# Merged per-tile orders, gates out of PSUM, fewer gathers and products of zeros in a 16-tile transformer kernel

## The reference

```python
h = ln(word[x] + pos[itok] + type[mask]) * gamma + beta            # E
h = h + relu((linear_attention(ln(h)) @ Wo.T + bo) @ Wfc.T + bfc)  # P: 16 heads, 44 random features each
h = h + experts(ln(h))                     # F: the two nearest of 32 prototypes, products of rank 16
h = h + rotary_attention(ln(h)) @ Wo                               # R: 16 heads, causal softmax
h = h + relu(ln(h) @ q(W1).T + b1) @ q(W2).T + b2                  # M: ternary weights, 256 to 1024 to 256
```

## Time and profile before

| | us |
|---|---|
| runs | 519.41, 523.40, 524.96 (median 523.4) |
| profiled execution | 519.33, with a span of 517.6 |
| TensorE busy | 394.7 (76%) |
| VectorE busy | 377.2 (73%) |
| GpSimd busy | 283.1 (55%) |
| ScalarE busy | 265.2 (51%) |
| mean granted TensorE clock | 0.91 |

### The profile page before, as it was taken

One profiled execution on the slowest core, in us unless ns is written; L12 is line 12 of the kernel. 1 busy time (PEld: TensorE's weight loads), 2 busy tenths in 40 slices (PEclk: granted clock), 3 DMA queues, 4 the chain that ended last, 5 costly groups with the idle time before them and its releaser, 6 DMA issues.

```text
span 517.6 us, 11583 instructions
## 1 busy us (share of the span) xinstructions
PE 394.7 (76%) x3722; PEld 261.4 (51%) x3754; DVE 377.2 (73%) x1026; ACT 265.2 (51%) x547; POOL 283.1 (55%) x380
## 2 busy tenths in 40 slices
PE   4164727587879888888988889889898988866764
PEld 1043414354546555655655557656565666443533
DVE  5254797889596979796969696979797977663231
ACT  2146532537383847474747474747565654624320
POOL 7516364658485758484848484848585534422110
PEclk9775567889897999999999999999999999988896
DMA  5587233464646696969596968886776858462472
GB/s 160 146 221 187 42 61 75 82 115 92 117 93 125 93 166 101 158 107 162 108 162 98 172 105 140 127 166 112 158 123 147 119 120 147 84 133 62 82 119 74
DMA packets 198650, 62.94 MB, mean 122 GB/s; under 512 B 190240, under 2 KB 195648, under 8 KB 198592
## 3 DMA queue, kind: packets, MB, share of 16 engines
q1 hardware_dynamic: 196288, 55.91, 59.1%
q0 software_dynamic: 2304, 6.29, 5.0%
HBM read 13.42 MB, written 2.10 MB: 30 GB/s over the span
## 4 chain that ended last, share of the span: by engine, by line
DVE 20%; POOL 17%; DMA 17%; PE 17%; issue 14%; SPq 12%; ACT 3%; POOLq 0%; DVEq 0%; ACTq 0%
DMA hgT<-hgs 7%; SPq L408 5%; PE PS L1241 5%; POOL stage_f L500 3%; PE PS L1341 3%; PE PS L1399 3%; SPq L418 2%; DMA xTr<-xsr 2%; POOL qe L528 2%; POOL split L508 2%; DMA rT<-split 2%; DMA mT<-stage_r 2%; POOL hres L504 2%; POOL rstdE L489 1%; POOL dist L522 1%
## 5 line engine op out<-in xcount | busy, mean ns | idle before, releaser
L1341 PE MATMUL PS<-w2q,mT 128*128 128x256 f16 x256 | 37.0, 308 | 5.7 <-DMA mT<-stage_r 5.7
L465 POOL TENSOR_TENSOR rstdR<-rstdR,consts 128x1 f32<-128x1 f32 x16 | 8.9, 559 | 55.8 <-DVE rstdR L926 55.8
L880 DVE TENSOR_REDUCE split<-PS 128x16 f16<-128x2048 f32 x16 | 36.5, 2284 | 3.7 <-PE PS L1327 3.7
L1241 PE MATMUL PS<-wqkT_hi,xTP 128*128 128x512 f16 x64 | 26.3, 456 | 14.3 <-DMA xTP<-xsP 14.3
L1318 PE MATMUL PS<-va,kp 128*88 128x34 f32 x256 | 25.6, 260 | 13.4 <-ACT kp L1192 13.4
L1592 PE MATMUL PS<-w1q,xTM 128*128 128x512 f16 x128 | 32.8, 379 | 2.3 <-DMA xTM<-xsM 1.5
L1399 PE MATMUL PS<-faT_hi,hgT 128*128 128x256 f16 x128 | 24.7, 281 | 12.8 <-DMA hgT<-hgs 12.2
L1318 PEld LDWEIGHTS PS<-va,kp 128*88 128x88 f32 x256 | 25.4, 178 | 17.4 <-ACT kp L1192 15.5
L1341 PEld LDWEIGHTS PS<-w2q,mT 128*128 128x128 f16 x256 | 26.9, 110 | 14.0 <-DMA mT<-stage_r 6.8
L1012 ACT ACTIVATE xnR<-hres,nmeanR,rstdR 128x256 f32<-128x256 f32 x16 | 9.6, 601 | 47.3 <-DVE nmeanR L938 47.3
L909 DVE SCALAR_TENSOR_TENSOR qs<-PS,qs 128x512 f16<-128x512 f32 x16 | 11.1, 691 | 28.2 <-ACT qs L1069 28.2
(11 more groups left out here) (282 smaller groups left out, 1428.5 us busy)
## 6 DMA issues: line engine op xcount, KB each, us to landing
out<-outb SPq DMA_DIRECT2D x16, 128.0 KB
w<-in_w1T SPq DMA_DIRECT2D x1, 1024.0 KB, 5.1
w<-in_w2T SPq DMA_DIRECT2D x1, 1024.0 KB, 8.0
stage_p<-in_wqkT SPq DMA_DIRECT2D x1, 512.0 KB, 3.7
stage_f<-in_fbT SPq DMA_DIRECT2D x1, 512.0 KB, 4.3
stage_f<-in_faT SPq DMA_DIRECT2D x1, 512.0 KB, 4.8
stage_r<-in_rwqk SPq DMA_DIRECT2D x1, 512.0 KB, 5.1
rT<-split SPq DMA_TRANSPOSE x32, 3.3
```

What stands on the lines that cost most here:

```text
L880: v.tensor_reduce(slots(48)[:, 0:H, 0].rearrange("p (c j) -> p j c", j=4), PS[:, BANK["mk1"]:BANK["mk1"] + 4, :].rearrange("p j (c k) -> p ...
L1241: last = pe.matmul(dst, xT[x][:, xp, :], wp[:, c, :], start=(n == 0), stop=(n == 3 * KC - 1 and bias is None))
L1341: pe.matmul(PS[:, BANK["m2"], 0:D], mT[:, j, :], w2q[:, j % FC, :], start=(j == 0), stop=False)
```

## The change

The step loop goes. Each engine's list is now all its ops for all 16 tiles, sorted by a place, `START[t] + STRETCH[t] * PLACE[op]`, and run from the first to the last. A place is a number for sorting; nothing waits for it. The semaphore waits are as before, except that TensorE's waits for a bank's earlier readers are written with counters (`issued`, `free`), the statistics use one semaphore less, and the banks are dealt anew. Laid out, the lists overlap more tiles: the gather runs five tiles ahead of fQ where it ran two ahead, and m2 seven behind.

Apart from that:

- Embedding: VectorE adds the two type rows to the 128 position rows once, SyncE writes the 256 x 256 sum to memory, and from tile 1 on each tile gathers from two tables instead of three; e1 is left out (tile 0 keeps three gathers and two adds, its first sum in `escaled`). The first gather of tile 1 waits for the table (`pt_out`).
- Gates: the row 0, 1, ..., 31 is written by a TensorE product into PSUM beside the distances of each tile, and the two comparisons read it there. The copy of the gates' high half goes to ScalarE (gsh, one instruction for both places), the low half to GpSimd (gsl). The sum of the weights and its reciprocal are an op of their own (ws). near moves from GpSimd to VectorE.
- Context: masked in place in PSUM; cth and ctl read it there.
- `keep_warm` issues products of zeros, 128x512 each, ahead of the wait of some products of tiles 0 to 4, into the bank that the product writes next. The entries for s1 in `WARM` are not used; the others are 48 products.

```diff
-LAG = {
-    "g": 0, "e1": 0, "e2": 0, "Est": 0, "Eag": 0, "Ers": 0, "Enm": 0, "Exn": 0,
-    "esc": 0, "eh": 0, "Pst": 0, "Pag": 0, "Prs": 0, "Pnm": 0, "Pxn": 0, "Phi": 0,
...
+FIRST, LAST = 3, 13
+START = (-2.56349, -1.38567, -0.20596, 0.99134, 2.22478, 3.48108, 4.78958, 6.10492, 7.46585, 8.85026, 10.27633, 11.72602, 13.22702, 14.73596, 16.29312, 17.86576)
+STRETCH = (0.87678, 0.89108, 0.90959, 0.9307, 0.95508, 0.97952, 0.99847, 1.02279, 1.04753, 1.07265, 1.09779, 1.12259, 1.14249, 1.16846, 1.20385, 1.2177)
+PLACE = {
+    "g": (-4.57909, -4.57909, -4.57909), "e2": (-3.97764, -3.97764, -3.97764), "Est": (-3.6722, -3.6722, -3.6722), "Eag": (-3.6282, -3.6282, -3.6282),
...
+    "PT": (-2.59489, -2.59489, -2.59489), "qk": (-0.58726, -0.58726, -0.58726), "v": (-0.25364, -0.25364, -0.25364), "qhi": (-0.31092, -0.31092, -0.31092),
...
+ENGINE = {
+    "SP": "PT qT qp onT hgT rT1 rT2 rT3 roT MT mT st".split(),
+    "POOL": "g e2 Ers esc eh Prs Plo qel onl Frs dist gsl hgl Rrs rot rl rol Mrs Mlo".split(),
+    "DVE": "Est Eag Enm Pst Pag Pnm qlo diag kmx kmr kb kd ctxt qmx qb qd ctl od on hP Fst Fag Fnm FT nd2 top near tix gap gt ws hg hF Rst Rag Rnm RT rc rs1 rs2 ngm rd ro hR Mst Mag Mnm ml1 ml2 ob".split(),
+    "ACT": "Exn Pxn Phi qhi sq ke kp va qe1 qe2 cth onh Fxn Fhi xsq tpf sec gsh hgh Rxn Rhi rh1 rh2 rh3 vr ex1 ex2 oh roh Mxn Mhi mh1 mh2".split(),
+    "PE": "qk v fK kmxT kbc ctx fQ o of Ftr prt fh y Rtr rqk rv mk1 s1 mk2 s2 pvx pvT wo m1 m2".split(),
+}
 BANK = {
-    "qk": 0, "kmxT": 2, "kbc": 6, "fK": 4, "v": 2, "ctx": 7, "fQ": 0, "o": 1,
-    "of": 1, "Ftr": 3, "prt": 3, "fh": 2, "y": 7, "Rtr": 7, "rqk": 7, "rv": 7,
-    "mk1": 3, "pvx": 6, "pvT": 7, "wo": 1, "m1": 0, "m2": 2,
+    "qk": 5, "kmxT": 7, "kbc": 6, "fK": 0, "v": 3, "ctx": 6, "fQ": 2, "o": 0,
+    "of": 3, "Ftr": 1, "prt": 7, "fh": 1, "y": 1, "Rtr": 3, "rqk": 3, "rv": 1,
+    "mk1": 4, "pvx": 4, "pvT": 0, "wo": 2, "m1": 2, "m2": 0,
 }
-TERN_BANK = 3
+
+
+WARM = {
+    "fQ": {0: 7, 1: 2},
+    "kmxT": {0: 5},
+    "ctx": {0: 2},
+    "o": {0: 3, 4: 1},
+    "of": {0: 10},
+    "kbc": {1: 1},
+    "Ftr": {0: 2},
+    "y": {0: 4, 2: 2, 3: 2},
+    "fK": {2: 4},
+    "s1": {0: 2, 1: 2},
+    "prt": {2: 1, 3: 2},
+}
+
+TERN_BANK = 4
...
+def due(engine):
+
+    def place(op, t):
+        return START[t] + STRETCH[t] * PLACE[op][0 if t < FIRST else 2 if t >= LAST else 1]
+
+    return sorted(((op, t) for op in ENGINE[engine] for t in range(TILES)), key=lambda x: (place(*x), x[1]))
 
...
-        emb = sb("emb", [P, 3, D])
-        esum1 = sb("esum1", [P, D])
+        emb = sb("emb", [P, 2, D])
+        emb_type = sb("emb_type", [P, D])
...
-        ctxt = sb("ctxt", [MP, HP, 2 * VA])
...
+            get("T", pos_rows, A["pos"])
+            get("T", pt_rows.rearrange("p r n -> p (r n)"), A["type"].partition_broadcast(P))
...
+            sp.wait_ge(pt_ok, 1)
+            sp.dma_start(A["pt"].rearrange("(r p) n -> p r n", p=P), pt_rows).then_inc(pt_out, 16)
...
-            for i in range(LAST_STEP + 1):
-                step(Step(i))
+            for op, t in due("SP"):
+                step(op, t)
...
+                if t == 1:
+                    g.wait_ge(ids_ok, 4)
+                    g.wait_ge(pt_out, 16)
+                tables = ((emb[:, 0, :], A["word"], ids[:, 0, t:t + 1]), (emb[:, 1, :], A["pos"], ids[:, 1, t:t + 1]),
+                          (emb_type[:, :], A["type"].rearrange("(r n) -> r n", n=D), ids[:, 2, t:t + 1]))
+                if t > 0:
+                    tables = (tables[0], (emb[:, 1, :], A["pt"], ids_pt[:, t:t + 1]))
+                for dst, table, rows_ in tables:
+                    g.indirect_dma_start(dst, None, table, bass.IndirectOffsetOnAxis(rows_, 0)).then_inc(g_ok, 16)
...
+                elif op == "gsl":
+                    wait(g, gsh_ok, t + 1)
+                    o = 2 * R2
+                    g.tensor_tensor(hgs[:, o + PROTO:o + 2 * PROTO], gates[:, :], hgs[:, o:o + PROTO], ALU.subtract).then_inc(gsl_ok, 1)
...
-                t = s.tile("gsp")
-                if t is not None:
-                    o = 2 * R2
-                    wait(v, gt_ok, 4 * t + 4)
-                    wait(v, hgT_ok, 16 * t)
-                    v.tensor_copy(hgs[:, o:o + PROTO], gates[:, :]).then_inc(gsp_ok, 1)
-                    v.tensor_copy(hgs[:, o + 2 * PROTO:o + 3 * PROTO], gates[:, :]).then_inc(gsp_ok, 1)
-                    wait(v, gsp_ok, 3 * t + 2)
-                    v.tensor_tensor(hgs[:, o + PROTO:o + 2 * PROTO], gates[:, :], hgs[:, o:o + PROTO], ALU.subtract).then_inc(gsp_ok, 1)
...
+                elif op == "near":
+                    wait(v, top_ok, t + 1)
+                    wait(v, dist_ok, t)
+                    v.tensor_scalar(near[:, :], top[:, 0:2], -1.0, None, ALU.mult).then_inc(near_ok, 1)
...
+                elif op == "ctxt":
+                    wait(v, ctx_ok, t + 1)
+                    ctxt = PS[0:MP, BANK["ctx"], 0:H * VA].rearrange("p (a b) -> p a b", a=HP)
+                    v.tensor_tensor(ctxt, ctxt, pair_mask[:, :, :], ALU.mult).then_inc(ctxt_ok, 1)
+                elif op == "ctl":
+                    wait(v, cth_ok, t + 1)
+                    v.tensor_tensor(ctl[:, :, :], PS[0:MP, BANK["ctx"], 0:H * VA].rearrange("p (a b) -> p a b", a=HP), cth[:, :, :],
+                                    ALU.subtract).then_inc(ctl_ok, 1)
...
+                elif op == "gt":
                     wait(v, sec_ok, t + 1)
                     wait(v, tpf_ok, t + 1)
-                    v.tensor_scalar(wsum[:, 0:1], second[:, :], 1.0, None, ALU.add).then_inc(gt_ok, 1)
-                    v.tensor_scalar(gate1[:, :], iota[:, :], topf[:, 1:2], second[:, 0:1], ALU.is_equal, ALU.mult).then_inc(gt_ok, 1)
-                    wait(v, gt_ok, 4 * t + 2)
-                    v.reciprocal(wsum[:, 1:2], wsum[:, 0:1]).then_inc(gt_ok, 1)
-                    v.scalar_tensor_tensor(out=gates[:, :], in0=iota[:, :], scalar=topf[:, 0:1], in1=gate1[:, :],
+                    wait(v, gsh_ok, t)
+                    wait(v, gsl_ok, t)
+                    order = PS[:, BANK["prt"], PROTO:2 * PROTO]
+                    v.tensor_scalar(gate1[:, :], order, topf[:, 1:2], second[:, 0:1], ALU.is_equal, ALU.mult).then_inc(gt_ok, 1)
+                    wait(v, gt_ok, 2 * t + 1)
+                    v.scalar_tensor_tensor(out=gates[:, :], in0=order, scalar=topf[:, 0:1], in1=gate1[:, :],
                                            op0=ALU.is_equal, op1=ALU.add).then_inc(gt_ok, 1)
...
+                elif op == "ws":
+                    wait(v, sec_ok, t + 1)
+                    v.tensor_scalar(wsum[:, 0:1], second[:, :], 1.0, None, ALU.add).then_inc(ws_ok, 1)
+                    wait(v, ws_ok, 2 * t + 1)
+                    v.reciprocal(wsum[:, 1:2], wsum[:, 0:1]).then_inc(ws_ok, 1)
...
+                elif op == "gsh":
+                    wait(a, gt_ok, 2 * t + 2)
+                    wait(a, hgT_ok, 16 * t)
+                    copy(hgs[:, 2 * R2:].rearrange("p (a b e) -> p a b e", a=2, b=2)[:, :, 0, :], gates[:, :].unsqueeze(1).to_broadcast([P, 2, PROTO]))\
+                        .then_inc(gsh_ok, 1)
...
+            issued = {product: 0 for product in BANK}
+            waited = {}
+
+            def free(name, sem_, readers):
+
+                if readers > waited.get(name, 0):
+                    pe.wait_ge(sem_, readers)
+                    waited[name] = readers
+
+            def keep_warm(name, t):
+                for _ in range(WARM[name].get(t, 0)):
+                    pe.matmul(PS[:, BANK[name], :], warm[:, 0:P], warm[:, :], start=True, stop=True)
+
             def masks(mask):
...
+                elif op == "fQ":
+                    free("qd_ok", qd_ok, t)
+                    free("ml1_ok", ml1_ok, issued["m1"])
+                    free("hR_ok", hR_ok, issued["wo"])
+                    free("ml2_ok", ml2_ok, issued["m1"])
+                    free("va_ok", va_ok, issued["v"])
+                    free("rope_ok", rope_ok, 3 * issued["rqk"])
+                    free("T_R", T_ok["R"], issued["Rtr"])
+                    free("hP_ok", hP_ok, issued["of"])
+                    keep_warm("fQ", t)
+                    wait(pe, qT_ok, 16 * (t + 1))
+                    features(BANK["fQ"], 0).then_inc(fQ_ok, 1)
+                    issued["fQ"] += 1
...
+                elif op == "prt":
+                    if t == 0:
+                        pe.wait_ge(v_set, 21)
+                    free("nd2_ok", nd2_ok, t)
+                    free("gt_ok", gt_ok, 2 * t)
+                    free("kmr_ok", kmr_ok, issued["kmxT"])
+                    free("ex2_ok", ex2_ok, issued["mk1"])
+                    keep_warm("prt", t)
+                    wait(pe, T_ok["F"], t + 1)
+                    pe.matmul(PS[:, BANK["prt"], PROTO:2 * PROTO], pick[:, :], iota_row[:, :], start=True, stop=True)
```

(3 more changed lines are left out.)

1472 lines of the change are left out of this document (668 added, 804 removed), and 21 rows, old and new, of tables (LAG, PLACE).

## The result

The changed kernel takes 528.7 us (median of 11 runs, 523.2 to 535.0) where the kernel before, run beside it, takes 524.6 (519.4 to 528.6). The ratio is 1.0082, 95% interval 1.0050 to 1.0113: slightly slower, within 1%. Its profiled execution is 528.48 with a span of 526.8, against 519.33 and 517.6 before. Forecast were 505 and a range of 485 to 528. Every later run is given by its median and by its ratio to the kernel before, run beside it (medians 524.4 to 526.4); the ratio leaves the slow executions of both out, so it can differ from that of the two medians, by 1.1% at most.

What follows compares the result with a forecast made beforehand. It took a ring of waits through in-order queues, 25.85 us a tile, as the bound. Steady -12.5, fill 0, products of zeros -2 and drain -2 took 519.3 to 502.8; 2 more for a median gave 505 us, range 485 to 528.

Steps and rivals of the forecast that it cites:

- the fill: Start of the run: first transpose 7.6 to 12 us later, regained by the fifth tile; booked 0, between -8 and +12.
- the products of zeros: 48 products ahead of TensorE's waits in the early tiles, to raise its clock: -2 us, between -6 and +2.
- the drain: End of the run, from y of tile 14: TensorE's old list, minus the casts: -2 us, 0 to -4.
- The steady stretch: Eleven tiles, fifth to last: new orders give 24.7 us a tile, 1.15 less; -12.5 us, between -38 and 0.
- the +1.3: Between y and s1: exponentials ahead of Rxn on ScalarE and Mrs ahead of rl on GpSimd add 1.3 us a tile.
- the 2.6: From s1 to the next y: TensorE's work 1.4 us shorter and two transpose waits, 1.2 us, gone, per tile.
- Gathers: GpSimd's embedding work: one gather of 1.01 us and two small instructions fewer a tile, hidden, so booked 0.
- the ring: Steady tiles: chain of waits through in-order queues, from y through s1 to the next y, 26.0 us against 25.85 measured.
- Gates: VectorE's gates: cast moved off, comparison reading PSUM, 1.7 us a tile off VectorE; nothing booked in the steady tiles.
- near: Scale moved from GpSimd to VectorE: 0.2 us taken, between 0.17 and 0.79 if held up by GpSimd.
- The wait of y: y's wait for its transposed operand hgT, to go because SyncE issues hgT before qp; 0.68 us a tile.
- Rival 3: The fill's delay stays: 528 us, chance 0.20; decides where the fill regains under 3 us and the tile stays above 25.5.

Runs made afterwards that it cites:

- rxn_early: cold_fill2_drain with Rxn of tiles 3 to 14 moved ahead of the previous tile's second exponential on ScalarE: 526.4 us, ratio 1.0046 to the kernel before.
- three_gathers: cold_fill2_drain with three gathers and two sums a tile as before, and no table of position and type sums: 532.9 us, ratio 1.0190.
- fill: The changed kernel with five instructions of tile 0 moved earlier on GpSimd, VectorE and ScalarE: 525.0 us, ratio 0.9987 to the kernel before.
- drain: The changed kernel with three instructions of tile 14 moved earlier on VectorE and ScalarE: 527.6 us, ratio 1.0012 to the kernel before.
- old_orders: The changed kernel's content with the orders and PSUM banks of the kernel before, without the 48 products of zeros: 522.9 us, ratio 1.0040.
- cold_fill2_drain: The changed kernel without the 48 products of zeros, ten instructions of tile 0 and three of tile 14 moved earlier: 518.1 us, ratio 0.9819.
- rag_early: cold_fill2_drain with Rag moved ahead of qd of two tiles on, tiles 2 to 13, on VectorE: 514.9 us, ratio 0.9860 to the kernel before.
- warm_later: cold_fill2_drain with only the 15 products of zeros of tiles 1 to 4: 518.0 us, ratio 0.9811 to the kernel before.
- no_warm: The changed kernel without its 48 products of zeros between the steps: 517.9 us, ratio 0.9877 to the kernel before.

## Why the prediction was wrong

The profiled pair was forecast 16.5 us apart to the one side and came out 9.2 apart to the other: 25.7 us off. By the first table 15.3 of them lie ahead of y of tile 3 (the fill 0 and the products of zeros -2 forecast, +13.3 measured), 8.3 in the drain (-2 and +6.3) and 2.1 in between.

*The steady stretch: the length right, the terms not.* -12.5 us over eleven tiles were forecast, 24.7 us a tile; it is 24.78, and 1.0 less over twelve tiles makes the -10.4 of the table. But the sum was 19.7 + 1.3 to the end of s1 and 2.6 less behind it. Averaged over tiles 4 to 11, y to the end of s1 takes 19.7 us in both kernels, and from there to the next y it is 6.1 before and 5.1 after. Neither the +1.3 nor more than 1.0 of the 2.6 came, and the two misses cancel: that the tile's length was hit is in part luck. Rxn lies behind the exponentials as said, and just as much behind Rnm (rxn_early): it starts 5.2 us behind y instead of 4.2, but rqk only 0.4 later, and by s1 this is made up. The transposes ahead of s1 did not land later.

*Gathers: 0 was wrong as an argument.* I said the ring hides GpSimd. In the new list the sum stands directly ahead of the rotary sum, and three_gathers shows about 1 us a tile hanging on it. The new lists with three gathers have tiles of 25.71, the old lists with the new content 25.39, the kernel before 25.80: by these single profiles neither part gives the 1.0 us alone, and the booking of the gain to TensorE's order alone was wrong. Orders and banks were only changed together, so what the new banks are worth is not known.

*Gates: right.* The comparison has a median of 310 ns (0.23 forecast, 789 before), the low half on GpSimd 246. *near: a median as forecast, and a tail.*

```profile
L863 DVE TENSOR_SCALAR gate<-PS,topf,second x16: 296/310/311, 84.7 to 454.7; 128x32 f32<-128x32 f32 x16
...
L848 DVE TENSOR_SCALAR near<-top x16: 168/169/1169, 82.4 to 451.8; 128x2 f32<-128x2 f32 x16
```

Twelve of its sixteen take 0.17 us, four take 0.87 to 1.17. The rule weighed in the prediction (the Trainium skill, SBUF — State Buffer, Who interferes with whom) speaks of such a lock, and the trace agrees: each of the four starts while GpSimd runs the low half of the rotary tile (rl, line 548) and ends 0.02 to 0.03 us behind it, and none of the twelve short ones starts in it. What they cost in time no run here shows. One of the four, from the two timelines:

```profile
285.87 1.16 POOL L548 TENSOR_TENSOR split<-stage_f,split 128x512 f16<-128x512 f32 x1 [0.23 <-ACT split L998]
...
286.18 0.87 DVE L848 TENSOR_SCALAR near<-top 128x2 f32<-128x2 f32 x1
```

*The wait of y: wrong.* It was to go and did not. Its group in the kernel before and in the changed one, count, busy us, mean ns, idle before:

```profile
L1399 PE MATMUL PS<-faT_hi,hgT 128*128 128x256 f16 x128 | 24.7, 281 | 12.8 <-DMA hgT<-hgs 12.2 <-issue 0.5
...
L1430 PE MATMUL PS<-faT_hi,hgT 128*128 128x256 f16 x128 | 25.3, 285 | 16.6 <-DMA hgT<-hgs 16.6
```

16.6 us over the run, where the kernel before has 12.2. What was saved behind s1 is TensorE's other work, not this wait.

*The fill and the products of zeros: the steps that failed.* The delay of the first transpose was worked out to 7.6 to 12 us and was 12.75 (2.1 of it in tile 0's own sum, which the prediction took as unchanged), and then I took it as regained by the fifth tile, on VectorE's idle time. y of tile 4 came at 196.4 against 184.0, over the 10 us that the prediction names as the sign of being wrong. Idle time of an engine is no cover when the work that would fill it stands behind another tile's in the same list: ScalarE's 5.74 us in the run fill are such idle time. By the ratios the early order costs about 5 us (fill against the changed kernel, booked 0), and the products of zeros 8 to 9 (booked -2, with +2 as the bad end). The sentence in brackets, ten products that can outlast the wait, was the right one; I priced it for a single group, and at the clock's possible gain (a clock above 0.85 between 25 and 130 us; it was 0.80) instead of the chain's loss. I had also not seen that the products themselves wait for the bank.

*The drain: wrong.* -2 was forecast, +6.3 measured. TensorE's list there is nearly the old one, but VectorE's and ScalarE's are not, and I had compared only TensorE's. The three moves of the run drain are not shown to matter, 1.4 us are m2 of tile 13 at the lower clock, and every kernel with the new content ends later than before's 57.6 us (58.4 to 63.9; old_orders, with its old lists, 60.3). What causes that stays open.

*Rivals.* Rival 3, 528, names the fill's delay and its number is the one measured, but its condition, a tile above 25.5, did not hold: the sum is the loss of the fill and the products, the steady gain and an unforeseen drain. That the number fits is luck. It is also counted from the lowest execution, without the 2 us for a median that the forecast adds.

*Still open:* why y of tile 3 stays 4 to 9 us later than before even with the first transpose at 25 and no products of zeros. With the old lists it was 5.2 later too, so part of it is in the content. There the sum of tile 0 ends 1.9 us later than before and the first transpose comes 2.3 later; three_gathers does not exclude the table of sums, and the rest was not tried.

*Better than both kernels:* cold_fill2_drain, 0.9819, ten moved instructions at the start, three at the end, and no products of zeros: 518.1 us beside 526.4 of the kernel before. rag_early, warm_later and no_warm, which moves nothing, measure the same within their intervals: leaving out the products is the only one of these steps that is clearly shown to pay.

## What to carry to other kernels

Before you book a change of order, walk every engine's list, SyncE's too, at the start, the middle and the end: in lists served in order, work of another tile ahead of the ring's instruction is on the ring, whatever the engine's idle share. Products that only keep a clock up do not fill a wait when the last wait comes before them: they are then work on the chain. In the first tile they cost 1.3% here, later nothing measurable, and no run showed the higher clock to buy time. Undo each part of a change alone: here a total of 0.8% hid one part that cost 1.8% and, by three_gathers, one that is worth 2% to 4%.

## What the runs showed of the hardware

A granted clock of 0.77 to 0.81 instead of 0.64 to 0.68 between 25 and 130 us came with a later y of tile 3 in each of the three pairs that differ by all 48 products of zeros (172.2 and 168.4, 174.3 and 173.1, 171.8 and 167.8). With the 15 later ones alone it was 0.75 instead of 0.66, and y of tile 3 came earlier (164.5 against 167.8). The 16 products of m2 of tile 13 took 1.91 to 1.92 us in the profiles of before, drain and no_warm, and 3.29 and 3.21 in those of the changed kernel and fill: 1.4 us of what single profiles differ by. That the queues of ScalarE, VectorE and GpSimd are kept strictly in order (the Trainium skill, PSUM — Partial Sum Buffer, Engine vs sequencer instructions) each timeline above agrees with: no instruction passed one that waited, and in the run fill ScalarE took up q and k of tile 0 only at 35.60, behind its 5.74 us of idle time, though TensorE had them done by 32.1.
